# Gate and up of the last two token blocks by seven half-depth products per chunk, with the last block's down products afterwards

## What is computed

```
x = x + layernorm(attention(layernorm(x)))     # 16 heads of 32, causal, with biases
x = x + layernorm(ffn(layernorm(x)))

def ffn(h):                                    # w_gate_up: 4096 x 512, w_down: 512 x 2048
    gate, up = split(h @ w_gate_up.T)          # 2048 features each
    return (silu(gate) * up) @ w_down.T
```

## Time and profile before

| | |
|---|---|
| median of three runs | 1066.56 us (1064.62 to 1066.61) |
| time of the profiled execution | 1062.67 us |
| its span, first to last instruction | 1060.6 us |
| TensorE busy | 1006.0 us (95% of the span), 5680 matmuls |
| VectorE busy | 671.5 us (63%) |
| ScalarE busy | 402.3 us (38%) |
| GpSimd busy | 617.9 us (58%) |
| mean granted TensorE clock | 0.984 of full speed |

### The profile page before, as it was taken

How to read it: one execution, slowest core, us unless ns; L and a number is a source line. 1 busy time by engine, 2 the same in 40 slices (tenths; PEclk the granted TensorE clock), 3 DMA queues, 4 the chain that set the end, 5 groups by cost and what they waited for, 6 DMA issues and landing times.

```text
span 1060.6 us, 16101 instructions
## 1 busy us (share of the span) xinstructions
PE 1006.0 (95%) x5680; PEld 776.4 (73%) x5680; DVE 671.5 (63%) x1215; ACT 402.3 (38%) x657; POOL 617.9 (58%) x353
## 2 busy tenths in 40 slices
...
GB/s 218 99 61 63 93 88 86 71 87 95 129 56 69 84 77 81 78 60 97 83 109 121 97 89 90 152 135 89 89 103 145 129 89 109 100 129 129 107 106 55
DMA packets 53052, 104.63 MB, mean 99 GB/s; under 512 B 10880, under 2 KB 11392, under 8 KB 52736
## 3 DMA queue, kind: packets, MB, share of 16 engines
...
q10 hardware_dynamic: 544, 0.26, 0.1%
...
## 4 chain that ended last, share of the span: by engine, by line
PE 77%; DVE 10%; POOL 6%; ACT 2%; issue 2%; DMA 1%; SPq 1%; POOLq 0%; ACTq 0%; DVEq 0%
PE ps L1258 19%; PE ps L1259 19%; PE ps L1260 19%; PE ps L1338 6%; PE ps L1372 5%; PE ps L1314 5%; POOL p_sum L610 2%; DVE ps L999 2%; PE ps L1386 1%; DVE p_sum L962 1%; DMA x_in<-x 1%; DVE xt_lo L976 1%; DVE stats L1137 1%; PE ps L1346 1%; DVE stats L1142 1%
## 5 line engine op out<-in xcount | busy, mean ns | idle before, releaser
L626 POOL TENSOR_TENSOR gu_lo<-gu_raw,gu_hi 128x1024 fp32r<-128x1024 f32 x64 | 153.9, 2405 | 219.3 <-ACT gu_hi L843 219.1
L999 DVE CUSTOM_DVE_ANT_0 ps<-ps,mask_q 128x384 f32<-128x384 f32 (+7 forms) x256 | 189.9, 779 | 70.2 <-PE ps L1314 67.3
L1258 PE MATMUL ps<-xt_hi,gu_hi 128*128 128x512 f32 x512 | 200.0, 391 | 0.0
L1259 PE MATMUL ps<-xt_lo,gu_hi 128*128 128x512 f32 x512 | 199.5, 390 | 0.0
L1260 PE MATMUL ps<-xt_hi,gu_lo 128*128 128x512 f32 x512 | 199.4, 390 | 0.0
L1109 DVE TENSOR_TENSOR h<-ps,silu 128x512 f32<-128x512 f32 x62 | 42.8, 690 | 228.0 <-PE ps L1260 222.3
L1115 DVE TENSOR_TENSOR h_lo<-h,h_hi 128x512 fp32r<-128x512 f32 x64 | 165.3, 2583 | 2.2
L1338 PE MATMUL ps<-q_stack,k_stack 98*128 98x512 f32 (+3 forms) x384 | 116.9, 382 | 6.5 <-DMA q_stack<-x_in 2.5
L632 POOL TENSOR_TENSOR dn_lo<-dn_raw,dn_hi 128x512 fp32r<-128x512 f32 x64 | 108.1, 1690 | 18.2 <-ACT dn_hi L850 18.2
L1314 PE MATMUL ps<-k_stack,q_stack 96*128 96x512 f32 (+3 forms) x384 | 109.8, 368 | 4.2 <-DVE m_full L999 2.9
L843 ACT ACTIVATE gu_hi<-gu_raw 128x1024 fp32r<-128x1024 f32 x64 | 67.8, 1061 | 117.8 <-PE ps L1260 117.8
...
## 6 DMA issues: line engine op xcount, KB each, us to landing
...
q_stack<-st_hi SPq DMA_DIRECT2D x128, 64.0 KB, 2.0
k_stack<-st_hi SPq DMA_DIRECT2D x128, 64.0 KB, 2.0
...
```

Of the source, the lines that this page charges most:

```text
L626: nc.gpsimd.tensor_tensor(gu_lo[:, s], gu_raw[:, s], gu_hi[:, s].bitcast(F32), ALU.subtract).then_inc(gu_split, 1)
L999: nc.vector.tensor_tensor_reduce(out=scores, in0=scores, in1=mask_q[:, SEQ - (t + 1) * P:], scale=1.0, scalar=MASKED, op0=ALU.add, op1=ALU ...
L1258: nc.tensor.matmul(dst, hi, r_hi, start=start, stop=False)
L1259: nc.tensor.matmul(dst, hi, r_lo, start=False, stop=False)
```

## The change

Blocks 0 and 1 stay as they are (`STD = 2`). Blocks 2 and 3 are worked on together, one chunk of weights for both. Seen as a 2x2 block product, with gate and up rows (G, U) against the two halves of the 512 features (0, 1), and the tokens X of block 2 and block 3 by the same halves, the chunk needs eight products of half depth. The changed kernel makes them from seven, by sums and differences of the operands (Winograd's form of Strassen's method): each product has 2 slices x 3 = 6 matmuls, so 42 per chunk for both blocks, where 2 x 24 = 48 stood.

- The weight sums `s_raw` (S1 to S4) are made by POOL for each chunk (`pair_weights`), `hi` and `lo` of them and of the three plain quarters that are used (`a_hi`, `a_lo`) too. The token sums T1 to T4 are made once, by POOL and ACT, during block 1 (`of_tokens`, `hi_of_tokens`).
- The seven results go to the banks 4, 6, 5, 7, 4, 5, 7 in that order (`pair_products`); after each of them DVE adds them up (`pair_hidden`; seven sums, then product, `hi` and `lo` for each block). ACT copies the first result out of bank 4 (`p_first`) and makes the two silus.
- Block 2's hidden activations are used at once by `down`, as before. Those of block 3 are kept for all 16 chunks in `xt` of batch 0 and in `hb_hi`, `hb_lo` (`of_b`), and their down products are a phase of their own (`down_b`), which adds up in the banks 4, 6, 5, 7 (`PAIR_OUT`). For it the down weights are loaded once more into quarters of the gate-and-up buffers (`b_weights`, four slots).
- The loads of gate-and-up weights fall from 64 to 48; those of down weights stay 64.

```diff
+PAIR_OUT = (4, 6, 5, 7)
+PER_PAIR, SUMS = 7, 7
+B_SLOTS = 4
...
+            def pair_weights(n):
+                s, c = n % 2, n - PAIR_N
+                raw = gu_raw[:, s].rearrange("p (k a n) -> p k a n", a=2, n=P)
+                pool.wait_ge(gu_loaded[s], DMA * (n // 2 + 1))
+                pool.wait_ge(gu_split, n)
+                nc.gpsimd.tensor_tensor(s_raw[:, S1], raw[:, 0:2, 1], raw[:, 2:4, 1], ALU.add).then_inc(s_made, 1)
+                nc.gpsimd.tensor_tensor(s_raw[:, S3], raw[:, 0:2, 0], raw[:, 0:2, 1], ALU.subtract).then_inc(s_made, 1)
+                pool.wait_ge(s_made, 4 * c + 1)
+                nc.gpsimd.tensor_tensor(s_raw[:, S2], s_raw[:, S1], raw[:, 0:2, 0], ALU.subtract).then_inc(s_made, 1)
+                pool.wait_ge(s_made, 4 * c + 3)
+                nc.gpsimd.tensor_tensor(s_raw[:, S4], raw[:, 2:4, 0], s_raw[:, S2], ALU.subtract).then_inc(s_made, 1)
+                pool.wait_ge(a_hi_done, 2 * c + 1)
+                nc.gpsimd.tensor_tensor(a_lo[:, s, 0:4], raw[:, :, 0], a_hi[:, s, 0:4].bitcast(F32), ALU.subtract)
+                pool.wait_ge(a_hi_done, 2 * c + 2)
+                nc.gpsimd.tensor_tensor(a_lo[:, s, 4:6], raw[:, 2:4, 1], a_hi[:, s, 4:6].bitcast(F32), ALU.subtract)
+                pool.wait_ge(s_hi_done, c + 1)
+                nc.gpsimd.tensor_tensor(gu_lo[:, s], s_raw.rearrange("p j k n -> p (j k n)"), gu_hi[:, s].bitcast(F32), ALU.subtract).then_inc(gu_split, 1)
...
+            def pair_chunk(c):
+                n = PAIR_N + c
+                act.wait_ge(pair_full, PER_PAIR * c + 1)
+                if c:
+                    act.wait_ge(pair_sum, SUMS * c - 2)
+                else:
+                    act.wait_ge(h_part, 2 * n - 1)
+                nc.scalar.activation(p_first, ps[:, 4], ACT.Copy).then_inc(first_copied, 1)
+                if c == 3:
+                    root(NORMS + BT * STD, 0, BT)
+                act.wait_ge(pair_sum, SUMS * c + 5)
+                act.wait_ge(h_part, 2 * n - 1)
+                nc.scalar.activation(silu[:, 0, :], ps[:, 4], ACT.Silu).then_inc(pair_silu, 1)
+                if c + 2 < CHUNKS:
+                    hi_of_pair(n + 2)
+                act.wait_ge(pair_sum, SUMS * c + 7)
+                nc.scalar.activation(ps[:, 7], ps[:, 7], ACT.Silu).then_inc(pair_silu, 1)
+                if c + 2 < CHUNKS:
+                    hi_of_sums(n + 2)
+                if c + 1 < CHUNKS:
+                    hi_of_dn(n + 1)
...
+            def pair_hidden(c):
+                n, s = PAIR_N + c, c % 2
+                vec.wait_ge(pair_full, PER_PAIR * c + 2)
+                vec.wait_ge(first_copied, c + 1)
+                nc.vector.tensor_tensor(u_sum, ps[:, 6], p_first, ALU.add).then_inc(pair_sum, 1)
+                vec.wait_ge(pair_full, PER_PAIR * c + 3)
+                vec.wait_ge(pair_sum, SUMS * c + 1)
+                nc.vector.tensor_tensor(v_sum, ps[:, 5], u_sum, ALU.add).then_inc(pair_sum, 1)
+                vec.wait_ge(pair_full, PER_PAIR * c + 4)
+                nc.vector.tensor_tensor(u_sum, ps[:, 7], u_sum, ALU.add).then_inc(pair_sum, 1)
+                vec.wait_ge(pair_sum, SUMS * c + 2)
+                nc.vector.tensor_tensor(w_sum[:, :], ps[:, 7], v_sum, ALU.add).then_inc(pair_sum, 1)
+                vec.wait_ge(pair_full, PER_PAIR * c + 5)
+                nc.vector.tensor_tensor(ps[:, 4], ps[:, 4], p_first, ALU.add).then_inc(pair_sum, 1)
+                vec.wait_ge(pair_full, PER_PAIR * c + 6)
+                nc.vector.tensor_tensor(ps[:, 5], ps[:, 5], v_sum, ALU.add).then_inc(pair_sum, 1)
+                vec.wait_ge(pair_sum, SUMS * c + 6)
+                vec.wait_ge(pair_silu, 2 * c + 1)
+                nc.vector.tensor_tensor(ps[:, 5], ps[:, 5], silu[:, 0, :], ALU.mult).then_inc(h_part, 1)
+                vec.wait_ge(h_part, 2 * n + 1)
+                vec.wait_ge(down_done, n - 1)
+                nc.vector.tensor_copy(h_hi[:, s, :], ps[:, 5]).then_inc(h_part, 1)
+                vec.wait_ge(h_part, 2 * n + 2)
+                nc.vector.tensor_tensor(h_lo[:, s, :], ps[:, 5], h_hi[:, s, :].bitcast(F32), ALU.subtract).then_inc(h_ready, 1)
+                vec.wait_ge(pair_full, PER_PAIR * c + 7)
+                nc.vector.tensor_tensor(ps[:, 7], ps[:, 7], u_sum, ALU.add).then_inc(pair_sum, 1)
+                vec.wait_ge(pair_silu, 2 * c + 2)
+                nc.vector.tensor_tensor(ps[:, 7], ps[:, 7], w_sum[:, :], ALU.mult).then_inc(b_part, 1)
+                vec.wait_ge(b_part, 2 * c + 1)
+                nc.vector.tensor_copy(of_b(c, True), ps[:, 7]).then_inc(b_part, 1)
+                vec.wait_ge(b_part, 2 * c + 2)
+                nc.vector.tensor_tensor(of_b(c, False), ps[:, 7], of_b(c, True).bitcast(F32), ALU.subtract).then_inc(b_ready, 1)
...
+            def pair_products(c, i=None):
+                n, s = PAIR_N + c, c % 2
+                def of_a(first):
+                    return a_hi[:, s, first:first + 2], a_lo[:, s, first:first + 2]
+                def of_s(j):
+                    return [buf[:, s].rearrange("p (j k n) -> p j k n", j=4, n=P)[:, j] for buf in (gu_hi, gu_lo)]
+                def of_x(j, half):
+                    return [buf[:, 1, 2 * j:2 * j + 2, half * BLK:(half + 1) * BLK] for buf in (xt_hi, xt_lo)]
+                def of_t(j):
+                    return t_hi[:, j], t_lo[:, j]
+                pe.wait_ge(gu_split, at(n + 1, 2, i))
+                if c:
+                    pe.wait_ge(pair_silu, at(2 * c - 1, 4, i))
+                else:
+                    pe.wait_ge(t_split, 4)
+                    pe.wait_ge(h_ready, n - 1)
+                product(4, of_a(0), of_x(0, 0))
+                if c:
+                    pe.wait_ge(pair_sum, at(SUMS * c - 6, 2 * SUMS, i))
+                product(6, of_s(S2), of_t(T2))
+                pe.wait_ge(h_ready, at(n, 2, i))
+                product(5, of_s(S3), of_t(T3))
+                if c:
+                    pe.wait_ge(b_ready, at(c, 2, i))
+                product(7, of_s(S1), of_t(T1))
+                pe.wait_ge(first_copied, at(c + 1, 2, i))
+                product(4, of_a(2), of_x(1, 0))
+                pe.wait_ge(pair_sum, at(SUMS * c + 2, 2 * SUMS, i))
+                product(5, of_a(4), of_t(T4))
+                pe.wait_ge(pair_sum, at(SUMS * c + 4, 2 * SUMS, i))
+                product(7, of_s(S4), of_x(1, 1))
+            def down_b(q, tiles=range(BT)):
+                if tiles[0] == 0:
+                    pe.wait_ge(b_ready, max(q + 1, CHUNKS if q == 0 and tiles[-1] == BT - 1 else 0))
+                    pe.wait_ge(b_split, q + 1)
+                for t in tiles:
+                    cols = slice(t * P, (t + 1) * P)
+                    last = three(ps[:, PAIR_OUT[t]], of_b(q, True)[:, cols], of_b(q, False)[:, cols], b_weights(gu_hi, q), b_weights(gu_lo, q),
+                                 q == 0, q == CHUNKS - 1)
+                    if q == CHUNKS - 1:
                         last.then_inc(out_full, 1)
-                if n < BLOCKS * CHUNKS - 1 and tiles[-1] == BT - 1:
-                    last.then_inc(down_done, 1)
+                if q < CHUNKS - 1 and tiles[-1] == BT - 1:
+                    last.then_inc(b_done, 1)
...
-                if blk + 1 < BLOCKS:
-                    down(blk, n0 + CHUNKS - 2, False, False)
+                down(blk, n0 + CHUNKS - 2, False, False)
+                if blk + 1 < STD:
                     gate_and_up(blk + 1, n0 + CHUNKS)
-                    down(blk, n0 + CHUNKS - 1, False, True)
-            n = BLOCKS * CHUNKS - 1
-            down(BLOCKS - 1, n - 1, False, False, tiles=range(BT - 1))
-            down(BLOCKS - 1, n, False, True, tiles=range(BT - 1))
-            down(BLOCKS - 1, n - 1, False, False, tiles=range(BT - 1, BT))
-            down(BLOCKS - 1, n, False, True, tiles=range(BT - 1, BT))
+                else:
+                    pair_products(0)
+                down(blk, n0 + CHUNKS - 1, False, True)
+            pair_products(1)
+            down(STD, PAIR_N, True, False)
+            with pe.Fori(0, CHUNKS // 2 - 2) as i:
+                for s in range(2):
+                    pair_products(2 + s, i)
+                    down(STD, PAIR_N + 1 + s, False, False, i)
+            pair_products(CHUNKS - 2)
+            down(STD, PAIR_N + CHUNKS - 3, False, False)
+            pair_products(CHUNKS - 1)
+            down(STD, PAIR_N + CHUNKS - 2, False, False)
+            down_b(0)
+            down(STD, PAIR_N + CHUNKS - 1, False, True)
+            for q in range(1, CHUNKS - 2):
+                down_b(q)
+            for tiles in (range(BT - 1), range(BT - 1, BT)):
+                for q in (CHUNKS - 2, CHUNKS - 1):
+                    down_b(q, tiles)
```

More of the change, by code:

```diff
@@ L542, in _ @@
                         load_dn(n0 + c, c, i)
+            for c in range(CHUNKS):
+                load_gu(PAIR_N + c, c)
+                load_dn(PAIR_N + c, c)
+                if c == 4:
+                    load_tiles(STD - 1)
```

(54 more changed lines are left out.)

189 lines of the change are left out of this document (166 added, 23 removed).

## The result

| | before | after | ratio, 95% interval |
|---|---|---|---|
| median | 1065.78 us (4 runs) | 1046.93 us (4 runs, 1044.16 to 1047.54) | 0.9828, 0.9811 to 0.9846 |
| measured once more, on another chip | 1065.38 us (9 runs) | 1045.27 us (7 runs, 1043.82 to 1049.83) | 0.9803, 0.9786 to 0.9819 |

A forecast was written before the change was run, and what follows sets the result against it. TensorE's matmul count and spacing were taken as the bound. Terms -21.8 - 0.3 + 2.9 + 0.2 gave -19.0 us, so 1047.6 us from the median 1066.56; range for 8 in 10: 1043.5 to 1053.

The forecast's parts named there:

- 96 matmuls: On TensorE, 6 of 48 matmuls go in each of 16 chunks, at 0.2267 us each: 21.8 us gained.
- The chain in a pair chunk: VectorE's thirteen steps at 0.73 us end at 14.95 us, before TensorE needs the bank at 16.32: no steady stop, 0.
- No hold-up by GpSimd: VectorE forms with a PSUM operand aren't held up by GpSimd instructions, so each was charged 0.73 us.
- Rival A: VectorE's sums wait out whole GpSimd instructions over the shared port: 37 us lost, 1085 us; chance 3%.
- Block 1: GpSimd's twelve added token-sum instructions during block 1 stay hidden behind TensorE: cost 0.
- Takeover and statistics: VectorE's takeover of block 1 and its statistics delay sums in early pair chunks: 0.1 us each.
- The new stop: TensorE's first down_b waits for bank 7, which block 3's last activations leave late: 2.9 us, bounds 2.3 and 3.8.
- The stop at the end: TensorE's last wait, for h_lo, goes because the last down products wait for no fresh activations: 0.3 us gained.
- The fall of the clock: TensorE's clock falls once after the stop before down_b, adding 1.6 us; chance 4 in 10.
- Rival B: Short stops at bank changes make TensorE's clock fall in every pair chunk: 26 us lost, 1073 us; chance 3%.
- Rivals C and D: C: slower VectorE steps or phase-edge stops lose 5 to 12 us, 9%; D: unseen wait, about 1066 us, 2%.

## Why the prediction was right, step by step

The mechanism was right, and each large term was met. That 18.9 us were measured for 19.0 forecast is closer than the terms are, and partly luck: by the trace they add up to 17.9, because the stop with its clock cost 4.2 where 2.9 stood in the sum, and the takeover nothing where 0.2 stood.

- **96 matmuls, 21.8 us.** Right: eight products in place of seven turn the gain into 4.9 us of loss, and the balance between first and last matmul closes to 0.1 us.
- **The chain in a pair chunk.** Right: `hb_lo` of the last chunk ends 14.65 us after its chunk began (975.97), 14.95 was worked out; the margin is 1.6 in place of 1.4. The steps are 0.67 to 0.70 long and 0.73 apart where one waits for the other, 0.60 where not, which the working didn't tell apart. One spare step fits, four cost 0.93 per chunk. Two side results of the working come out otherwise when redone: with 0.95 per step a chunk would lose some 0.7 us, not 1, and with 0.62 the new stop would be 2.0 us, not 2.3.
- **No hold-up by GpSimd.** Right for the forms used, and the experiment with SBUF operands shows that the form decides it: 6.6 us are lost again. Rival A's mechanism is real, but for operands that the change doesn't use there. Its price of 37 us assumed two hold-ups, together 3.7 us, in every chunk; the steady chunk has one, of 2.1.
- **Block 1, 0 us.** Right, with `h_lo` at 2.69 us on average (2.77 in the same stretch before); with most of the token sums made twice, 7.3 us were lost there.
- **Takeover and statistics, 0.2 us.** Mis-sized: 0. The first sum behind the takeover begins 4.7 us into its chunk (809.33; the chunk began at 804.61) where 5.2 was worked out, and the next ones stand 0.60 apart in place of 0.73 (810.12, 810.72, 811.32), so sum 4 is over at 7.4, and 8.16 would have done.
- **The new stop, 2.9 us.** 2.6, within the bounds: the last chain was 0.3 us shorter.
- **The stop at the end, 0.3 us.** Right; TensorE has no distance over 0.26 us there any more.
- **The fall of the clock, 4 in 10, 1.6 us, left out of the sum.** The chance was set too low. It came in four of the five profiles in which TensorE stopped for 2.7 to 3.3 us there (both of the changed kernel, eight products, one spare step), not in the fifth (doubled token sums), and in both with a longer stop. With it in the sum the forecast would have been 1049.2, and the medians, 1046.9 and 1045.3, lie on the other side of 1047.6: 1.6 us can't be told from the scatter of the attention part.
- **Rival B**, the clock falling in every chunk: no. The granted clock is 1.00 from 600 to 975 us, though the banks now change every six matmuls. **Rivals C and D**: nothing of them.

The chance for the fall rested on "idle times of 2 us passed without one". In the trace of the kernel before TensorE was idle for some 2 us three times from 440 us on: 446.22 to 448.26, 471.12 to 473.15 and 540.81 to 542.73. The first and the third passed without a fall, the second did not (the granted clock is the third number from the end), so that trace already showed both outcomes:

```profile
446.00:448.00 2.00, 0.22 (x1) 0.00 (x0) 1.88 (x7) 0.47 (x1) 1.90 (x1) 1.00 0.45 111
...
472.00:474.00 2.00, 0.85 (x13) 0.55 (x17) 1.26 (x6) 1.25 (x2) 1.86 (x2) 0.92 0.00 0
474.00:476.00 2.00, 2.00 (x28) 1.14 (x24) 0.00 (x0) 0.00 (x0) 1.92 (x2) 0.50 0.06 16
```

What stays open: why the attention part ends up to 7 us earlier or later with the same instructions, and what decides whether a stop of 2.7 us brings a fall.
